# One kernel, one change: equal-width attention passes, high probabilities first, and the addition of the two halves moved behind the gate rows

## The chip, the cores and the metric

The kernel runs on one core of one Trainium2 chip. The metric is the device time of one execution in microseconds (us). TensorE does the matrix products, VectorE (DVE in the profile), ScalarE (ACT) and GpSimd (POOL) the work on elements, SyncE (SP) starts most transfers. Each engine takes its instructions in the order in which they are written; between engines only semaphores hold the order.

## The reference, cut to what matters

Eight sequences of 512 tokens with 256 features go through a state-space block (stage A), a mixture-of-experts attention with 16 heads of 64 features (stage B) and a feed-forward block (stage C). The change is in stage B:

```
q = rope(x Wq); k = rope(x Wk)
v = sum over experts e of gv[e] * (x Wv[e])
att = softmax(q k^T / 8)
o = att v
out = sum over experts e of (go[e] * o) Wo[e]
```

The products are kept near fp32 accuracy by splitting each operand into a high part (rounded for TensorE) and a low part (what the rounding left). A product is then high x high + high x low + low x high.

## The kernel before, in words

Stage B runs 64 times over one body: 8 pairs of heads (`j`) times 8 sequences (`b`), `it = 8 j + b`, called a batch here. Each engine has its own `batch` function, and these four lists of calls, written out by hand, are the schedule.

For one batch TensorE (`batch`, L1169) makes the values of both heads (`values`), the scores (`scores`), then transposes the probabilities of head 0 (`turn_probabilities`, L1107, n = 0 to 3), multiplies values by probabilities for head 0 (`attend`, L1124), does the same for head 1 (n = 4 to 7) with the transpose of the output gates between (`turn_gates`), spreads the gates over all partitions (`spread_gates` p = 0 to 3, L1138), with the next batch's q and k between them (`project_raw`), and ends with the eight steps of the output product (`project` n = 0 to 7, L1149). `project` n = 0 waits for `oT_low0`, the low part of the first gated output.

Each transposed block of probabilities is split: ScalarE writes the high part (`high_probabilities`, L1241), VectorE the low part (`low_probabilities`, L1366, waits for the high part). `probT` has four places, so head 1 uses those of head 0 again; ScalarE waits for `pv_psum` of the pass that read the place.

`attend` forms, for a head and a block c of 128 keys, two passes of 512 columns into one PSUM bank. The tile `vv` holds a head's values as 64 high columns and then 64 low columns. The pass with the high probabilities takes all 128 columns and so fills 128 PSUM partitions: high values in one half, low values in the other. The pass with the low probabilities takes only the 64 high columns and adds to the first half. Both wait until the low probabilities of block c are there:

```
pe.wait_ge(pT_low, it * N + n + 1)
```

The output of a head is the sum of the two halves of its bank. ScalarE copies one half to the partitions of the other, into the tile `aside` (`move_part`, L1251), and VectorE adds it (`add_parts`, L1378) into `oT`. `move_part` waits for the four passes of its head and for `oT_done`, which `add_parts` counts up:

```
act.wait_ge(pv_psum, it * N + h * TT + TT)
act.wait_ge(oT_done, it * 2 + h)
```

So `move_part` of head 1 comes behind `add_parts` of head 0.

VectorE's list for this part of a batch is: low probabilities 0 to 3, `output_gates`, one step of the ranking of gates (`tops`), `add_parts` of head 0, low probabilities 4 to 7, `low_gates` (L1371, the low part of the transposed gates, 16 rows from partition 64 on), `add_parts` of head 1, `gate_outputs` 0 and 1 (L1385, gate times `oT`), and more. `gate_outputs` 0 waits for both `add_parts`. ScalarE then makes `ogT_high` (`high_outputs`, L1258) and GpSimd `ogT_low` (`low_outputs`, L971) of the first four gated outputs, for which `project` waits.

GpSimd sums the gated expert values in `sum_values` (L956) through the tile `qk_full`, whose second half (`qk_full[:, 1, :]`) holds the sums of the later tokens (`v4`). `rotate` (L1330) writes the whole of `qk_full` for the next batch.

Of the kernel before, what the change touches and what calls it, by code (L numbers as in the profile page):

```python
# [15 lines left out]
F32, F32R = mybir.dt.float32, mybir.dt.float32r  # L16
ALU = mybir.AluOpType
ACT = mybir.ActivationFunctionType
AX = mybir.AxisListType

P = 128
NB, S, D = 8, 512, 256
TT = S // P
# [6 lines left out]
H, E, HP, F = 16, 8, 64, 1024  # L30
# [758 lines left out]
def stage_b(nc, d, const, acc):  # L789
# [6 lines left out]
    with ExitStack() as ctx:  # L796
        def sb(name, shape, dtype=F32):
            return ctx.enter_context(nc.sbuf_tensor(name, shape, dtype))
# [7 lines left out]
        ps = ctx.enter_context(nc.psum_tensor("ps_b", [P, 8, S], F32))  # L806
# [23 lines left out]
        qk_full = sb("qk_full", [P, 2, S])  # L830
# [1 line left out]
        vg = sb("vg", [P, TT, E, HP])  # L832

        v4 = qk_full[:, :, :].rearrange("p a s -> p (a s)").rearrange("p (t e n) -> p t e n", t=TT, e=E // 2)
        oT, aside = sb("oT", [P, S]), sb("aside", [P, S])
        v2 = sb("v2", [P, TT, E // 4, HP])
        v = sb("v", [P, 2, TT, HP])
        vv = sb("vv", [P, 2, TT, 2 * HP], F32R)
        negmax = sb("negmax", [P, TT, 2])
        total = sb("total", [P, 2, TT])  # L840
        share = sb("share", [P, 2, TT])
# [3 lines left out]
        RING = 4  # L845
# [22 lines left out]
        N = BLOCKS  # L868
# [58 lines left out]
        def turns(eng, start, batch, pair_start=None):  # L927

            def pair(j, more):
                if pair_start:  # L930
                    pair_start(j)
                with eng.Fori(0, NB - 1) as b:
                    batch(j * NB + b, j, b, True, False)
                batch(j * NB + (NB - 1), j, NB - 1, False, more)

            start()
            with eng.Fori(0, PAIRS - 1) as j:
                pair(j, True)
            pair(PAIRS - 1, False)

        @block.gpsimd
        def _(pool):
            def low_x(it):
                pool.wait_ge(xT_high, it + 1)
                pool.tensor_tensor(xT[1][:, :, :], xT_in[:, :, :], xT[0][:, :, :].bitcast(F32), ALU.subtract).then_inc(xT_low, 1)
# [20 lines left out]

            def low_values(it, h):
                pool.wait_ge(v_high, it * 2 + h + 1)
                pool.tensor_tensor(vv[:, h, :, HP:2 * HP], v[:, h, :, :], vv[:, h, :, 0:HP].bitcast(F32), ALU.subtract).then_inc(v_low, 1)

            def low_outputs(it, e):  # L971

# [85 lines left out]
                    rank_four(it + 1, ahead)  # L1058

            pool.memset(out_gate[:, :, :], 0.0).then_inc(zero_done, 1)  # L1060
            low_x(0)

            pool.dma_start(acc[:, :, :, :], d["xT"].rearrange("b p k s -> p b k s")).then_inc(acc_loaded, 16)
# [3 lines left out]
        def _(pe):  # L1067
# [53 lines left out]
                    mm = pe.transpose(ps[:, GT_BANK, t * P:(t + 1) * P], out_gate[:, t, :], ident[:, :])  # L1121
                mm.then_inc(gT_psum, 1)

            def attend(it, h, c):  # L1124

                if c == 0:
                    pe.wait_ge(v_low, it * 2 + h + 1)
                n = h * TT + c
                pe.wait_ge(pT_low, it * N + n + 1)
                bank, last = ATTEND_BANK[h], c == TT - 1  # L1130
                if last:
                    pe.matmul(ps[0:HP, bank, :], vv[:, h, c, 0:HP], probT[1][:, n % RING, :], start=False, stop=False)
                mm = pe.matmul(ps[:, bank, :], vv[:, h, c, :], probT[0][:, n % RING, :], start=(c == 0), stop=last)
                if not last:
                    mm = pe.matmul(ps[0:HP, bank, :], vv[:, h, c, 0:HP], probT[1][:, n % RING, :], start=False, stop=False)
                mm.then_inc(pv_psum, 1)

            def spread_gates(it, p):  # L1138

# [29 lines left out]
            def batch(it, j, b, more, more_pairs):  # L1169
                pe.wait_ge(w_low["wv"], j * 2 + 2)  # L1170
                values(it, 0, 0)
                values(it, 0, 1)
                scores(it, 0)
                scores(it, 1)
                values(it, 0, 2)
                values(it, 0, 3)
                values(it, 1, 0)
                scores(it, 2)
                scores(it, 3)
                values(it, 1, 1)  # L1180
                values(it, 1, 2)
                values(it, 1, 3)
                for n in range(TT):
                    turn_probabilities(it, n)
                for c in range(TT):
                    attend(it, 0, c)
                for n in range(TT, N):
                    turn_probabilities(it, n)
                turn_gates(it)
                for c in range(TT):  # L1190
                    attend(it, 1, c)
                spread_gates(it, 0)
                spread_gates(it, 1)
                if more or more_pairs:
                    if more_pairs:
                        pe.wait_ge(w_low["wqk"], j + 2)
                    project_raw(it + 1, 0)
                spread_gates(it, 2)
                if more or more_pairs:
                    project_raw(it + 1, 1)  # L1200
                spread_gates(it, 3)
                for n in range(N):
                    project(it, j, n)

            pe.wait_ge(consts_done, 1)
            turns(pe, start, batch)

        @block.scalar
        def _(act):
# [26 lines left out]

            def high_values(it, h):
                act.wait_ge(vsum_done, CREDIT + it * VSUM + h * 6 + 6)
                act.activation(vv[:, h, :, 0:HP], v[:, h, :, :], ACT.Copy).then_inc(v_high, 1)

            def high_probabilities(it, n):  # L1241
                act.wait_ge(pT_psum, it * N + n + 1)
# [74 lines left out]
        def _(dve):  # L1317
# [12 lines left out]
            def rotate(it):  # L1330

                dve.wait_ge(vsum_done, CREDIT + it * VSUM)
                dve.wait_ge(rot_done, it * 3 + 3)
                dve.tensor_tensor(qk_full[:, :, :], rot[:, 0:2, :], rot[:, 2:4, :], ALU.add).then_inc(qk_done, 1)

# [35 lines left out]
            def low_gates(it):  # L1371

                dve.wait_ge(gT_high, it + 1)
                rows = slice(LOW_ROW, LOW_ROW + 2 * E)
                low = gT[rows, :]
                dve.tensor_tensor(low, ps[rows, GT_BANK, :], low.bitcast(F32), ALU.subtract).then_inc(gT_low, 1)

            def add_parts(it, h):  # L1378

                here = slice(h * HP, (h + 1) * HP)  # L1380
                dve.wait_ge(part_moved, it * 2 + h + 1)
                dve.wait_ge(og_done, CREDIT + it * EP)
                dve.tensor_tensor(oT[here, :], ps[here, ATTEND_BANK[h], :], aside[here, :], ALU.add).then_inc(oT_done, 1)
# [37 lines left out]
            def batch(it, j, b, more, more_pairs):  # L1421
                coming = (it + 1, j if more else j + 1, b + 1 if more else 0)
                gate_values(it, j, b, 0)
                maxima(it, 0)
                maxima(it, 1)
                gate_values(it, j, b, 1)
                maxima(it, 2)
                maxima(it, 3)
                gate_values(it, j, b, 2)
                gate_values(it, j, b, 3)  # L1430
                for n in range(TT):
                    low_probabilities(it, n)
                output_gates(it)
                if more or more_pairs:
                    tops(*coming, 0)
                add_parts(it, 0)
                for n in range(TT, N):
                    low_probabilities(it, n)
                low_gates(it)
                add_parts(it, 1)  # L1440
                gate_outputs(it, 0)
                gate_outputs(it, 1)
                if more or more_pairs:
                    tops(*coming, 1)
                gate_outputs(it, 2)
                gate_outputs(it, 3)
                if more or more_pairs:
                    turn_raw(it + 1)
                low_outputs(it, 0)
                if more or more_pairs:  # L1450
                    swap_halves(it + 1)
                low_outputs(it, 1)
                if more:
                    tops(*coming, 2)
                if more or more_pairs:
                    rotate(it + 1)
                low_outputs(it, 2)
                low_outputs(it, 3)
                if more_pairs:
                    tops(*coming, 2)  # L1460
                    low_qk(it + 1)
                    tops(*coming, 3)
                elif more:
                    tops(*coming, 3)
                    low_qk(it + 1)
                dve.wait_ge(acc_loaded, 16)
                dve.wait_ge(out_psum, CREDIT + it * KD + KD)
                dve.tensor_tensor(acc[:, bass.ds(b, 1), :, :], acc[:, bass.ds(b, 1), :, :], ps[:, OUT:OUT + KD, :].unsqueeze(1),
                                  ALU.add).then_inc(acc_done, 1)

            dve.wait_ge(tables_loaded, 32)
            dve.wait_ge(consts_done, 1)
            dve.wait_ge(zero_done, 1)
            turns(dve, start, batch)


# [394 lines left out]
```

## Time and profile before

| | us |
|---|---|
| median of 3 runs | 4357.75 (4352.01 to 4357.77) |
| the profiled execution | 4360.78 |
| its span, first to last instruction | 4358.8 |
| TensorE busy | 3803.9 (87%) |
| VectorE busy | 3630.8 (83%) |
| GpSimd busy | 2849.6 (65%) |
| ScalarE busy | 2029.6 (47%) |
| mean granted TensorE clock over the span | 0.909 of 2.4 GHz |

Stage B lies between about 1450 and 4080 us of the span. A matmul is pipelined: the record of one lasts longer than the step to the next one's start, so steps are read from starts. An engine's "idle before" is the time since its last instruction ended, with the instruction that ended the wait. "issue" is idle time for which the profile shows no releaser.

### The profile page before, as it was taken

What the parts mean: (1) busy time and instruction counts of PE and PEld (TensorE: products, weight loads), DVE (VectorE), ACT (ScalarE), POOL (GpSimd) and SP (SyncE); (2) the same over time, 40 slices, a digit from 0 to 9 for tenths busy, and PEclk for the clock granted to TensorE, in tenths of its full rate; (3) what the DMA queues carried; (4) which work ended last, traced back from release to release, by engine and by line L of the source; (5) the groups of instructions that cost most, each with busy time, mean ns of one, the idle gap of its engine ahead of it and who ended that gap; (6) DMA issues with size and microseconds to landing.
All of it is one profiled execution on the core that took longest, in us unless ns stands there. A gap on an engine that the chain in (4) does not pass through costs nothing. (4 is left out here: it accounts for less than half of the span.)

```text
span 4358.8 us, 54031 instructions
## 1 busy us (share of the span) xinstructions
PE 3803.9 (87%) x15744; PEld 2541.1 (58%) x15744; DVE 3630.8 (83%) x4012; ACT 2029.6 (47%) x3761; POOL 2849.6 (65%) x2524
## 2 busy tenths in 40 slices
PE   6777867867765599999999999999999999999787
PEld 2233323323322377777777777777777777777676
DVE  5999999999998478877887887887888788778598
ACT  4544535535443244544444444444444444444433
POOL 2758668567594366766766766766766766766444
PEclk8877877877876799999999999999999999999898
DMA  1000000000000300100100100100100100000101
GB/s 39 0 10 15 24 5 19 24 5 19 15 5 20 131 13 12 41 14 10 41 14 10 41 14 10 41 14 10 41 14 10 41 14 10 20 14 15 31 29 44
DMA packets 48726, 97.83 MB, mean 22 GB/s; under 512 B 3570, under 2 KB 33138, under 8 KB 46228
## 3 DMA queue, kind: packets, MB, share of 16 engines
q1 hardware_dynamic: 47620, 92.94, 6.2%
q0 software_dynamic: 1040, 4.19, 0.2%
q8 instruction: 19, 0.31, 0.0%
q14 instruction: 47, 0.39, 0.0%
HBM read 80.34 MB, written 16.78 MB: 22 GB/s over the span
## 5 line engine op out<-in xcount | busy, mean ns | idle before, releaser
L702 DVE TENSOR_TENSOR_SCAN state<-dA,dBx 128x2048 f32<-128x2048 f32 x128 | 726.8, 5678 | 25.9 <-POOL y_part L289 21.3
L1234 ACT ACTIVATE prob<-ps_b,negmax 128x512 f32<-128x512 f32 x512 | 346.1, 687 | 652.3 <-DVE negmax L1353 652.3
L286 POOL TENSOR_TENSOR state<-state,c_copy 128x1024 f32<-128x1024 f32 x120 | 345.5, 2879 | 374.8 <-DVE state L702 374.8
L1347 DVE TENSOR_TENSOR vg<-ps_b,gates 128x1024 f32<-128x1024 f32 x256 | 313.5, 1224 | 253.1 <-PE ps_b L1072 241.1
L961 POOL TENSOR_TENSOR qk_full<-vg 128x512 f32<-128x512 f32 x256 | 329.0, 1285 | 253.3 <-DVE vg L1347 253.3
L549 ACT ACTIVATE dA<-dt,a_neg 128x511 f32<-128x511 f32 x512 | 326.9, 711 | 323.9 <-DVE state L702 323.7
L974 POOL TENSOR_TENSOR ogT_low<-prob,ogT_high 128x512 fp32r<-128x512 f32 x256 | 324.0, 1295 | 208.9 <-ACT ogT_high L1267 208.9
L372 PE MATMUL ps_a<-xp_high,ident_r 33*128 33x512 f32 x256 | 163.0, 637 | 332.6 <-DVE dBx L692 307.9
L1070 PE MATMUL ps_b<-ogT_high,wo_high 128*128 128x512 f32 x1024 | 413.2, 403 | 11.1 <-DVE ogT_low L1399 10.8
L1070 PE MATMUL ps_b<-wv_high,xT_high 128*128 128x512 f32 x1024 | 414.6, 405 | 0.0
L289 POOL TENSOR_TENSOR y_part<-y_part,state 128x1024 f32<-128x1024 f32 x120 | 403.4, 3362 | 9.4
L1072 PE MATMUL ps_b<-ogT_high,wo_low 128*128 128x512 f32 x1024 | 405.2, 396 | 0.0
L1071 PE MATMUL ps_b<-ogT_low,wo_high 128*128 128x512 f32 x1024 | 402.9, 393 | 0.0
L1071 PE MATMUL ps_b<-wv_low,xT_high 128*128 128x512 f32 x1024 | 401.5, 392 | 0.0
L1072 PE MATMUL ps_b<-wv_high,xT_low 128*128 128x512 f32 x1024 | 399.2, 390 | 0.0
L393 PE MATMUL ps_a<-state,ident 128*128 128x512 f32 x512 | 345.9, 813 | 24.8 <-DVE work L719 22.7
L1353 DVE TENSOR_REDUCE negmax<-ps_b 128x2 f32<-128x1024 f32 x256 | 301.0, 1217 | 62.8 <-PE ps_b L1103 62.8
L372 PEld LDWEIGHTS ps_a<-xp_high,ident_r 33*128 33x128 f32 x256 | 59.0, 231 | 495.5 <-DVE dBx L692 399.0
L1368 DVE TENSOR_TENSOR probT_low<-ps_b,probT_high 128x512 fp32r<-128x512 f32 x512 | 316.4, 677 | 2.3 <-ACT probT_high L1245 2.3
L1245 ACT ACTIVATE probT_high<-ps_b 128x512 fp32r<-128x512 f32 x512 | 264.7, 605 | 61.8 <-PE ps_b L1114 59.7
L692 DVE TENSOR_TENSOR dBx<-du,ps_a 128x2048 f32<-128x2048 f32 x128 | 289.0, 2258 | 1.8 <-PE ps_a L373 1.8
L1267 ACT ACTIVATE ogT_high<-ps_b 128x512 fp32r<-128x512 f32 x256 | 153.1, 598 | 242.0 <-PE ps_b L1072 242.0
(237 smaller groups left out, 9530.9 us busy)
## 6 DMA issues: line engine op xcount, KB each, us to landing
xT<-xT_scratch SPq DMA_DIRECT2D x65, 512.0 KB, 3.3
wv<-in_wv SPq DMA_DIRECT2D x8, 1024.0 KB, 4.9
wo<-in_wo SPq DMA_DIRECT2D x8, 1024.0 KB, 7.0
x_in<-in_x SPq DMA_DIRECT2D x8, 512.0 KB, 4.7
x_a<-in_x SPq DMA_DIRECT2D x8, 512.0 KB, 5.3
x_scratch<-x_a SPq DMA_DIRECT2D x8, 512.0 KB, 2.9
xT_scratch<-x2T SPq DMA_DIRECT2D x8, 512.0 KB, 2.6
scores_scratch<-sg SPq DMA_DIRECT2D x8, 512.0 KB, 3.5
```

The costliest lines, as they stand in the source:

```text
L286: pool.tensor_tensor(state, state, c, ALU.mult).then_inc(hc_part_done, 1)
L289: pool.tensor_tensor(y[:, :, :], y[:, :, :], state, ALU.add).then_inc(y_part_done, 1)
L393: mm = pe.matmul(ps[:, m, :], ident[:, :], h[n % 2][:, m, :], start=(n == 0), stop=(n == NS - 1))
L549: act.activation(dA[n % 2][:, m, 1:S], dt[par][:, m, 1:S], ACT.Exp, scale=a_neg[:, m, n:n + 1]).then_inc(dA_done, 1)
L702: dve.tensor_tensor_scan(h[n % 2][:, :, :].rearrange("p c s -> p (c s)"), dA[n % 2][:, :, :].rearrange("p c s -> p (c s)"), dBx[n % 2][:, ...
L961: pool.tensor_tensor(v4[:, at, :, :], vg[:, at, 0:4, :], vg[:, at, 4:8, :], ALU.add).then_inc(vsum_done, 1)
L974: pool.tensor_tensor(ogT[1][:, e, :], og[:, e, :], ogT[0][:, e, :].bitcast(F32), ALU.subtract).then_inc(oT_low0, 1)
L1070: pe.matmul(out, left(0), right(0), start=start, stop=False)
L1071: pe.matmul(out, left(0), right(1), start=False, stop=False)
L1072: return pe.matmul(out, left(1), right(0), start=False, stop=stop)
L1234: act.activation(prob[h][:, t, :], ps[:, score_bank(t) + h, :], ACT.Exp, bias=negmax[:, t, h:h + 1], accum_out=total[:, h, t:t + 1]).then_ ...
L1368: dve.tensor_tensor(probT[1][:, n % RING, :], ps[:, n % TT, :], probT[0][:, n % RING, :].bitcast(F32), ALU.subtract).then_inc(pT_low, 1)
```

## The change

The tile `vv` gets 64 more columns per block that are always zero, and its order becomes low, high, zero. The pass with the high probabilities takes low and high, that with the low probabilities high and zero, so all passes are 128 columns wide. `attend` does a whole head: four passes with the high probabilities, each waiting only for the high part of its block (`pT_high`), and then four with the low ones, each waiting for `pT_low`; each low pass counts `pv_psum`. As VectorE's progress is no longer implied by the first wait, `attend` waits for `vg_done` as well. `aside` has no tile of its own any more: it lies in the second half of `qk_full`, and `rotate` waits for `oT_done`. GpSimd zeroes the new columns once, and TensorE and VectorE wait for that at the start of the stage. On VectorE `add_parts` of head 0 moves from before low probabilities 4 to 7 to behind `low_gates`. `move_part` and `add_parts` themselves are as before.

```diff
-        oT, aside = sb("oT", [P, S]), sb("aside", [P, S])
+        oT, aside = sb("oT", [P, S]), qk_full[:, 1, :]
...
-        vv = sb("vv", [P, 2, TT, 2 * HP], F32R)
+        vv = sb("vv", [P, 2, TT, 3 * HP], F32R)
...
             def low_values(it, h):
                 pool.wait_ge(v_high, it * 2 + h + 1)
-                pool.tensor_tensor(vv[:, h, :, HP:2 * HP], v[:, h, :, :], vv[:, h, :, 0:HP].bitcast(F32), ALU.subtract).then_inc(v_low, 1)
+                pool.tensor_tensor(vv[:, h, :, 0:HP], v[:, h, :, :], vv[:, h, :, HP:2 * HP].bitcast(F32), ALU.subtract).then_inc(v_low, 1)
...
             pool.memset(out_gate[:, :, :], 0.0).then_inc(zero_done, 1)
+            pool.memset(vv[:, :, :, 2 * HP:3 * HP].bitcast(F32), 0.0).then_inc(zero_done, 1)
             low_x(0)
...
-            def attend(it, h, c):
-
-                if c == 0:
-                    pe.wait_ge(v_low, it * 2 + h + 1)
-                n = h * TT + c
-                pe.wait_ge(pT_low, it * N + n + 1)
-                bank, last = ATTEND_BANK[h], c == TT - 1
-                if last:
-                    pe.matmul(ps[0:HP, bank, :], vv[:, h, c, 0:HP], probT[1][:, n % RING, :], start=False, stop=False)
-                mm = pe.matmul(ps[:, bank, :], vv[:, h, c, :], probT[0][:, n % RING, :], start=(c == 0), stop=last)
-                if not last:
-                    mm = pe.matmul(ps[0:HP, bank, :], vv[:, h, c, 0:HP], probT[1][:, n % RING, :], start=False, stop=False)
-                mm.then_inc(pv_psum, 1)
+            def attend(it, h):
+
+                pe.wait_ge(v_low, it * 2 + h + 1)
+                pe.wait_ge(vg_done, it * 4 + 3)
+                bank = ATTEND_BANK[h]
+                for c in range(TT):
+                    pe.wait_ge(pT_high, it * N + h * TT + c + 1)
+                    pe.matmul(ps[:, bank, :], vv[:, h, c, 0:2 * HP], probT[0][:, c % RING, :], start=(c == 0), stop=False)
+                for c in range(TT):
+                    pe.wait_ge(pT_low, it * N + h * TT + c + 1)
+                    pe.matmul(ps[:, bank, :], vv[:, h, c, HP:3 * HP], probT[1][:, c % RING, :], start=False, stop=(c == TT - 1)).then_inc(pv_psum, 1)
...
-                for c in range(TT):
-                    attend(it, 0, c)
+                attend(it, 0)
                 for n in range(TT, N):
                     turn_probabilities(it, n)
                 turn_gates(it)
-                for c in range(TT):
-                    attend(it, 1, c)
+                attend(it, 1)
...
             pe.wait_ge(consts_done, 1)
+            pe.wait_ge(zero_done, 2)
...
             def high_values(it, h):
                 act.wait_ge(vsum_done, CREDIT + it * VSUM + h * 6 + 6)
-                act.activation(vv[:, h, :, 0:HP], v[:, h, :, :], ACT.Copy).then_inc(v_high, 1)
+                act.activation(vv[:, h, :, HP:2 * HP], v[:, h, :, :], ACT.Copy).then_inc(v_high, 1)
...
             def rotate(it):
 
                 dve.wait_ge(vsum_done, CREDIT + it * VSUM)
+                dve.wait_ge(oT_done, it * 2)
...
-                add_parts(it, 0)
                 for n in range(TT, N):
                     low_probabilities(it, n)
                 low_gates(it)
+                add_parts(it, 0)
                 add_parts(it, 1)
                 gate_outputs(it, 0)
...
-            dve.wait_ge(zero_done, 1)
+            dve.wait_ge(zero_done, 2)
```

## Rows read from the trace of the kernel before

**Rows 1.** Busy time by stretch: PE, PEld, DVE, ACT, POOL, clock, DMA, GB/s.
```profile
1700.00:4200.00 2500.00, 2431.05 (x11816) 1817.19 (x11814) 1986.33 (x2603) 1192.93 (x2420) 1710.45 (x2002) 0.99 0.06 22
```

**Rows 2.** Waits between 1704.58 and 4023 us: total us, times, longest.
```profile
PEld ps_b L1133 <- DVE probT_low L1368: 130.3, 348, 1.4
```

**Rows 3.** TensorE in order of time, one batch: start us, us, operation.
```profile
3001.99 1.91 PE L1114 MATMUL ps_b<-ident,prob 128*128 128x128 f32 x16
...
3006.13 0.45 PE L1132 MATMUL ps_b<-probT_low,vv 128*64 128x512 f32 x1
3006.41 0.40 PE L1133 MATMUL ps_b<-probT_high,vv 128*128 128x512 f32 x1
3006.85 1.20 PE L1147 MATMUL ps_b<-gT,spread 128*128 128x512 f32 x4
...
3011.13 0.63 PE L1147 MATMUL ps_b<-gT,spread 128*128 128x512 f32 x2
3011.69 0.47 PE L1070 MATMUL ps_b<-ogT_high,wo_high 128*128 128x512 f32 x1
```

**Rows 4.** What ended TensorE's idle time before L1147: us, times.
```profile
  DVE gT L1376: 30.4, 64
```

**Rows 5.** VectorE in order of time, the same batch.
```profile
2998.95 2.48 DVE L1368 TENSOR_TENSOR probT_low<-ps_b,probT_high 128x512 fp32r<-128x512 f32 x4
...
3003.00 0.68 DVE L1383 TENSOR_TENSOR oT<-ps_b,aside 64x512 f32<-64x512 f32 x1 [0.79 <-ACT aside L1256]
3003.61 2.47 DVE L1368 TENSOR_TENSOR probT_low<-ps_b,probT_high 128x512 fp32r<-128x512 f32 x4
3006.11 0.69 DVE L1376 TENSOR_TENSOR gT<-ps_b,gT 16x512 fp32r<-16x512 f32 x1
3007.55 0.69 DVE L1383 TENSOR_TENSOR oT<-ps_b,aside 64x512 f32<-64x512 f32 x1 [0.76 <-ACT aside L1256]
```

**Rows 6.** ScalarE in order of time, the same batch.
```profile
2998.17 2.07 ACT L1245 ACTIVATE probT_high<-ps_b 128x512 fp32r<-128x512 f32 x4 [1.05 <-PE ps_b L1114]
...
3001.81 0.42 ACT L1239 ACTIVATE vv<-v 128x256 fp32r<-128x256 f32 x1 [0.63 <-POOL v L965]
3002.27 0.60 ACT L1256 ACTIVATE aside<-ps_b 64x512 f32<-64x512 f32 x1
3002.89 2.07 ACT L1245 ACTIVATE probT_high<-ps_b 128x512 fp32r<-128x512 f32 x4
...
3006.93 0.59 ACT L1256 ACTIVATE aside<-ps_b 64x512 f32<-64x512 f32 x1 [1.47 <-PE ps_b L1133]
3009.53 2.28 ACT L1267 ACTIVATE ogT_high<-prob 128x512 fp32r<-128x512 f32 x4 [2.02 <-DVE prob L1392]
```

**Rows 7.** GpSimd between 3010.3 and 3011.3 us.
```profile
3010.24 1.30 POOL L974 TENSOR_TENSOR ogT_low<-prob,ogT_high 128x512 fp32r<-128x512 f32 x1 [3.24 <-ACT ogT_high L1267]
```

**Rows 8.** GpSimd, then TensorE, in the last batch, between 4059 and 4062 us.
```profile
4060.10 2.55 POOL L974 TENSOR_TENSOR ogT_low<-prob,ogT_high 128x512 fp32r<-128x512 f32 x2 [4.70 <-ACT ogT_high L1267]
...
4061.54 0.47 PE L1070 MATMUL ps_b<-ogT_high,wo_high 128*128 128x512 f32 x1 [0.26 <-POOL ogT_low L974]
```

**Rows 9.** Weight loads of L1132 and L1133: ns min/median/max, first and last start.
```profile
L1132 PEld LDWEIGHTS ps_b<-probT_low,vv x128: 132/133/133, 1508.3 to 4056.1; 128*64 128x64 f32 x128
...
L1133 PEld LDWEIGHTS ps_b<-probT_high,vv x512: 186/186/189, 1506.5 to 4056.1; 128*128 128x128 f32 x171
```

**Rows 10.** GpSimd in order of time at the start of stage B.
```profile
1447.04 0.52 POOL L1060 MEMSET out_gate<- 128x512 f32 x1 [34.49 <-POOLq L123]
1455.42 2.34 POOL L945 TENSOR_TENSOR xT_low<-xT,xT_high 128x1024 fp32r<-128x1024 f32 x1 [7.85 <-ACT xT_high L1213]
```

**Rows 11.** ScalarE, then VectorE, in a pair's first batch, 3443.9 to 3445 us.
```profile
3443.86 0.60 ACT L1245 ACTIVATE probT_high<-ps_b 128x512 fp32r<-128x512 f32 x1
...
3444.49 0.69 DVE L1368 TENSOR_TENSOR probT_low<-ps_b,probT_high 128x512 fp32r<-128x512 f32 x1 [0.34 <-ACT probT_high L1245]
```

**Rows 12.** VectorE between 3008.3 and 3009.3 us, the batch of rows 5.
```profile
3008.28 1.22 DVE L1392 TENSOR_TENSOR prob<-oT,ps_b 128x1024 f32<-128x1024 f32 x1
```

## The prediction, made before the result was known

> **What bounds the kernel now.** I read the page first: its busy shares and its list of groups. The change touches stage B alone. By stretches, TensorE is busy 2431 of 2500 us there at a granted clock of 0.99, that is at its upper level, 2.4 GHz, while VectorE has 1986 us [rows 1]. So a batch (64 of them, some 40 us each) lasts as long as TensorE's passes plus its few stalls, and the question is which stalls the change shortens or adds. The list of waits names the ones aimed at: passes of L1133 waiting for low probabilities, 130.3 us over 348 times, as weight loads [rows 2].
>
> Next I followed one batch in order of time, TensorE, VectorE, ScalarE and GpSimd side by side. The reader is to see that what ends each stall is a chain through other engines, not the passes:
>
> - Head 0: VectorE's fourth low part ends at 2998.95 + 2.48 = 3001.43, and TensorE goes on to the transposes of head 1 at 3001.99 [rows 3, 5].
> - ScalarE's `move_part` of head 0 starts at 3002.27, right behind the rounding of head 1's values, and that waited for GpSimd's sum [rows 6]. Not the attention passes but the value sums set when it starts. Then come ScalarE's high parts 4 to 7, from 3002.89.
> - VectorE: `add_parts` 0 from 3003.00 to 3003.68, low parts 4 to 7 from 3003.61 to 3006.08, `low_gates` from 3006.11 to 3006.80 [rows 5]. TensorE's gate spreading starts at 3006.85 [rows 3]; it waited for `low_gates` in all 64 batches, 30.4 us [rows 4]. The last pass of head 1, started at 3006.41, was early enough.
> - The second half: ScalarE `move_part` 1 from 3006.93 to 3007.52, VectorE `add_parts` 1 at 3007.55, `gate_outputs` 0 at 3008.28, `ogT_high` at 3009.53, GpSimd's `ogT_low` from 3010.24 to 3011.54, `project` at 3011.69 [rows 3, 5, 6, 7, 12].
> - Is that last wait real? TensorE's previous pair of passes, 3011.13 with 0.63 us in all, starts its second pass 0.23 us after its first (a record lasts 0.40 us) and would let `project` begin at 3011.13 + 2 x 0.23 = 3011.59. It began 0.10 us later, 0.15 us after GpSimd's end. In the last batch, where TensorE has nothing else to do, the trace names this releaser: GpSimd ends at 4060.10 + 1.30 = 4061.40 and `project` starts 0.14 us later [rows 7, 8]. The same handing over, so `project` is held by this chain in every batch, with TensorE only 0.10 us behind it.
>
> **The change part by part.**
>
> *Order of the passes.* Head 0: the fourth low part still ends at 3001.43; one pass stands behind it where there were two, so the transposes begin at most one step (0.23 us) sooner. Nothing downstream takes that up: `move_part` 0 is held by GpSimd's sums. I take 0; the ends are 0 and -0.23 us a batch. Head 1: the last pass is released by the fourth low part and followed by none, but the gates' spreading waits for `low_gates` anyway. The new waits: `vg_done` 3 and `v_low` are over long before, so they cost 0.
>
> *Width.* A low pass now loads 128 columns of weights, 186 ns for 133 [rows 9]; only loads that follow a wait are exposed, and at most the difference, 0.05 us, for each head. It falls in front of `low_gates`' end, so 0.
>
> *Zeroing and tile.* A fill of 512 elements per partition takes 0.52 us, once, and GpSimd then idles 7.85 us for ScalarE [rows 10]: 0; uncovered it would be 0.5 us in all. `rotate` comes some 10 us after `add_parts` 1 on its own engine: 0. `aside` in `qk_full` is written by ScalarE after the last value sum: 0.
>
> *`add_parts` 0 behind `low_gates`.* This is the dear part. Ahead of it there is a small gain: low part 4 no longer waits behind the addition, but for its high part, which ends at 3002.89 + 0.60 = 3003.49. A low part that waits only for that starts 0.03 us after it (3443.86 + 0.60 = 3444.46, then 3444.49) [rows 11]. So 3003.52 for 3003.61; the four end at 3005.99, `low_gates` at 3006.02 + 0.69 = 3006.71, and TensorE's spreading starts near 3006.76, 0.09 us sooner.
>
> Behind it stands a loss. `move_part` 1 still waits for `add_parts` 0, which so far was long done, and which now comes last:
> - `add_parts` 0 behind `low_gates`: 3006.71 + 0.03 = 3006.74, ends at 3007.42 (0.68 us).
> - ScalarE takes it up 0.03 us later (`gate_outputs` 0 ends at 3008.28 + 1.22 = 3009.50, `ogT_high` starts at 3009.53) [rows 6, 12]: `move_part` 1 from 3007.45 to 3008.04. Its passes have been over since about 3006.5.
> - `add_parts` 1 0.03 us later, at 3008.07 instead of 3007.55: **0.52 us late**.
>
> Behind `move_part` 1 in ScalarE's order are only the `high_outputs`, which need its result anyway. From `add_parts` 1 to `project` everything is a chain of the same lengths: `gate_outputs` 0, `ogT_high`, `ogT_low` move by 0.52, and `project` starts at 3012.21. The gate spreading p = 3 waits for `gate_outputs` 1, at most 3008.28 + 2 x 1.22 + 0.52 = 3011.24, and is through by 3011.9; it is not the last. Behind `project` 0 the passes follow each other, so all else shifts with it. Cost: 64 x 0.52 = 33.3 us.
>
> *Both ends of the unknowns.* The step from `low_gates` to `add_parts` 0 isn't in the trace. Low parts that follow each other start 0.07 us before the one in front ends (four of 0.67 us in 2.47: a step of 0.60); `low_gates` behind a low part started 0.03 us after its end, and `gate_outputs` 0 behind `add_parts` 1 at 3008.24 + 0.04 [rows 5, 12]. In these two the start partition changes, from 0 to 64 and back, as it will here. So 0.03; with the overlap the batch costs 0.42 us and the sum is 27 us. The Trainium skill, "VectorE: DVE Perf Modes", section "Two Vector instructions with no wait between them", says that an instruction whose inputs or output start in another quadrant than the last ones starts only when all earlier ones have finished; the trace agrees (0.03 us after the end against 0.07 before it), and by the page the sum is 33 us where free overlap would give 27. Handing over from ScalarE took 0.03 us for `move_part` 1 but 0.13 for `move_part` 0 (3002.87 to 3003.00) [rows 5, 6]. I take 0.03, since `move_part` 1 is the same instruction with ScalarE idle behind it; two such dearer steps would make 0.72 us, 46 us. If TensorE were not ready for `project` on time it would change nothing, for it is ready 0.6 us before.
>
> **The sum.** The profiled execution took 4360.78 us, 3.03 above the median. 4360.78 + 33.3 = 4394.1, and by the median 4357.75 + 33.3 = **4391 us**.
>
> **The rivals.**
>
> *TensorE's order decides (faster).* TensorE has the highest busy share, so passes that no longer wait in pairs should tell. In head 1 the last pass would be released near 3006.05 and the spreading could begin near 3006.38 rather than at 3006.41 + 0.23 = 3006.64: 0.26 us, 64 x 0.26 = 17 us, 4341. This holds if neither `low_gates` nor GpSimd's end really releases TensorE. Against it: 64 waits out of 64 at L1147, and the named releaser in the last batch. It decides as soon as the chain behind `add_parts` 1 has over 0.6 us of slack.
>
> *The late addition is hidden (no change).* GpSimd's spans are rough; if `project` were held by something else than `ogT_low`, the 0.52 us would vanish and the 0.09 us before the spreading remain: 4357.75 - 6 = 4352. For it speaks that the trace files this wait of TensorE's under "issue" in ordinary batches; against it the equal 0.15 and 0.14 us.
>
> *Dearer handings over (slower still).* 0.13 us at both of ScalarE's ends: 4404.
>
> *The clock.* TensorE idles some 0.9 us more per batch in single stalls of up to 0.7 us. Were a tenth of each batch's passes granted 1.2 GHz, some 4 us of steps would double: over 250 us in all. In this stretch the clock stayed at 0.99 with stalls of 0.3 to 0.5 us each batch, so I give it little.
>
> **How the numbers follow.** Forecast 0.80 (own range 4384 to 4398), dearer steps 0.05, clock 0.02, hidden 0.07, faster 0.06. A measurement of this kernel can tell about 0.2% (8.7 us) from no change. Slower by more: 0.80 + 0.05 + 0.02 = 0.87; within: 0.07; faster by more: 0.06. The range for 8 in 10 takes the forecast's own range, the dearer steps as far as 4402, and some room below for a part that is hidden: 4379 to 4402.
>
> **What would show it.** `add_parts` 1 starting 9.12 us after the batch's first low part (3008.07 - 2998.95) where it was 8.60, `move_part` 1 released by VectorE's `oT` instead of TensorE; `low_gates` ending 0.09 us sooner; the first `ogT_low` 0.5 us late and TensorE's wait at L1070 growing from 0.10 to near 0.7 us; a batch of 40.5 us. The prediction is wrong if `project` starts on time although `ogT_low` is late, if the clock row falls, or if `move_part` 1 isn't released by `add_parts` 0.

## The result, and the profile after

| | before | after |
|---|---|---|
| median, us | 4354.9 (4352.01 to 4357.77, 4 runs) | 4387.41 (4385.64 to 4390.99, 4 runs) |
| profiled execution, us | 4360.78 | 4386.21 |
| its span, us | 4358.8 | 4384.0 |

The ratio is 1.0076, 95% interval 1.0058 to 1.0093: 33 us slower (25 to 41). The forecast was +33.3 us and 4391; the 4391 stood on the median of three runs, 4357.75, and by the median in this table the same 33.3 us give 4388.

Read the profile after in the same order. First VectorE in order of time over one batch (start, length in us, operation; "L1367" is `low_probabilities`, L1375 `low_gates`, L1382 `add_parts`, L1391 `gate_outputs`):

```profile
3013.26 2.48 DVE L1367 TENSOR_TENSOR probT_low<-ps_b,probT_high 128x512 fp32r<-128x512 f32 x4
...
3017.83 2.48 DVE L1367 TENSOR_TENSOR probT_low<-ps_b,probT_high 128x512 fp32r<-128x512 f32 x4 [1.31 <-ACT probT_high L1243]
3020.34 0.69 DVE L1375 TENSOR_TENSOR gT<-ps_b,gT 16x512 fp32r<-16x512 f32 x1
3021.06 0.68 DVE L1382 TENSOR_TENSOR oT<-ps_b,qk_full 64x512 f32<-64x512 f32 x1
3022.40 0.69 DVE L1382 TENSOR_TENSOR oT<-ps_b,qk_full 64x512 f32<-64x512 f32 x1 [0.66 <-ACT qk_full L1254]
```

Beside [rows 5], counted from the batch's first low part: the four low parts of head 1 start at 4.57 us (4.66 before), `low_gates` ends at 7.77 (7.85), and `add_parts` 1 starts at 9.14 (8.60; forecast 9.12). The small gain in front and the large loss behind it are both there. Who holds `add_parts` 1 is seen on ScalarE:

```profile
3016.13 0.42 ACT L1237 ACTIVATE vv<-v 128x256 fp32r<-128x256 f32 x1 [0.64 <-POOL v L965]
3016.58 0.59 ACT L1254 ACTIVATE qk_full<-ps_b 64x512 f32<-64x512 f32 x1
3017.20 2.06 ACT L1243 ACTIVATE probT_high<-ps_b 128x512 fp32r<-128x512 f32 x4
...
3021.78 0.59 ACT L1254 ACTIVATE qk_full<-ps_b 64x512 f32<-64x512 f32 x1 [2.03 <-DVE oT L1382]
```

`move_part` 1 starts at 3021.78, 0.04 us after `add_parts` 0 ends (3021.06 + 0.68), and its releaser is VectorE's `oT`; before it was TensorE's last pass [rows 6]. By the totals of the line:

```profile
L1254 ACT ACTIVATE qk_full<-ps_b x128: 589/594/597, 1503.9 to 4085.6; 64x512 f32<-64x512 f32 x128
its engine sat idle before it (us, times) until:
  DVE oT L1382: 129.8, 64
```

All 64 times the new wait ended last. On TensorE (L1132 the passes with high, L1135 those with low probabilities, L1146 the spreading, L1071 the first pass of `project`):

```profile
3018.22 1.58 PE L1132 MATMUL ps_b<-probT_high,vv 128*128 128x512 f32 x4
3019.65 1.22 PE L1135 MATMUL ps_b<-probT_low,vv 128*128 128x512 f32 x4
3021.09 1.20 PE L1146 MATMUL ps_b<-gT,spread 128*128 128x512 f32 x4 [0.22 <-DVE gT L1375]
...
3025.54 0.72 PE L1146 MATMUL ps_b<-gT,spread 128*128 128x512 f32 x2
3026.53 0.47 PE L1071 MATMUL ps_b<-ogT_high,wo_high 128*128 128x512 f32 x1 [0.27 <-POOL ogT_low L974]
```

The passes of head 1 end sooner (their last starts by 3020.4, 1.4 us before `move_part` 1), and nothing comes of it. `project` now waits visibly: GpSimd's `ogT_low` is the named releaser, where the trace before filed the wait under "issue" [rows 3, 8]. By the totals of L1071 it is the releaser in all 64 batches:

```profile
  POOL ogT_low L974: 16.9, 64
```

Last, the stretch as a whole: `low_gates` first and last start.

```profile
L1375 DVE TENSOR_TENSOR gT<-ps_b,gT x64: 689/689/690, 1507.7 to 4084.1; 16x512 fp32r<-16x512 f32 x64
```

From the first to the last of its 64 the kernel before took 4056.0 - 1512.9 = 2543.1 us and this one 2576.4: 33.3 us more in 63 batches, 0.53 each. The spans differ by only 25.2 us because the rest, whose code is the same but for one fill, was 8 us shorter in this profiled run. In what follows this distance ("first to last gate") is the measure in a trace.

Busy times and granted clock (the third column from the end) over nearly all batches, of the kernel before and then after:

```profile
1510.00:4040.00 2530.00, 2492.28 (x12026) 1851.20 (x12024) 2022.77 (x2570) 1206.30 (x2473) 1762.55 (x2103) 1.00 0.06 20
1510.00:4040.00 2530.00, 2482.93 (x11877) 1864.04 (x11876) 2001.77 (x2536) 1193.36 (x2447) 1742.33 (x2077) 1.00 0.06 20
```

The clock is 1.00 in both: in the profiled executions the added stalls cost none. Over the whole span it was 0.908 to 0.910 in three of the four runs after, and 0.87 in the fourth, which took 4390.99 us, 2.4 more than the next; that run has no trace, so where its clock was lower isn't known.

### The profile page after: what moved, and what is told of

Same layout as the page of the kernel before. It is cut to its first block and busy times, and to the rows that moved or that the text cites. A ratio compares the mean times of both kernels' runs of the same rounds, so it can differ in the third digit from the quotient of the medians.

```text
span 4384.0 us, 54159 instructions
## 1 busy us (share of the span) xinstructions
PE 3829.7 (87%) x15744; PEld 2578.2 (59%) x15744; DVE 3628.0 (83%) x4012; ACT 2030.9 (46%) x3761; POOL 2854.5 (65%) x2525
## 5 line engine op out<-in xcount | busy, mean ns | idle before, releaser
L1071 PE MATMUL ps_b<-ogT_high,wo_high 128*128 128x512 f32 x1024 | 409.4, 400 | 27.7 <-POOL ogT_low L974 16.9
L1071 PE MATMUL ps_b<-wv_high,xT_high 128*128 128x512 f32 x1024 | 414.4, 405 | 0.0
L1367 DVE TENSOR_TENSOR probT_low<-ps_b,probT_high 128x512 fp32r<-128x512 f32 x512 | 317.5, 683 | 91.1 <-ACT probT_high L1243 91.1
L393 PE MATMUL ps_a<-state,ident 128*128 128x512 f32 x512 | 355.4, 832 | 24.8 <-DVE work L719 22.6
```

The lines of the kernel that those rows point to most:

```text
L393: mm = pe.matmul(ps[:, m, :], ident[:, :], h[n % 2][:, m, :], start=(n == 0), stop=(n == NS - 1))
L1071: pe.matmul(out, left(0), right(0), start=start, stop=False)
L1367: dve.tensor_tensor(probT[1][:, n % RING, :], ps[:, n % TT, :], probT[0][:, n % RING, :].bitcast(F32), ALU.subtract).then_inc(pT_low, 1)
```

## The experiments

The theory: the whole cost is that `move_part` 1 waits for `add_parts` 0. The rivals: the passes (their order or width) or the shared tile cost something; or the place of the addition on VectorE costs by its own length.

**e1: the addition back in its place.**

```diff
+                add_parts(it, 0)
                 for n in range(TT, N):
                     low_probabilities(it, n)
                 low_gates(it)
-                add_parts(it, 0)
                 add_parts(it, 1)
```

> The changed kernel with add_parts 0 back before low probabilities 4 to 7; passes, zero columns and tiles stay changed. Theory (the late addition in front of move_part 1 is the whole cost): add_parts 1 starts 8.60 us after the batch's first low part again, project 1 starts as in the kernel before, time within 0.2% of the kernel before, about 4355 to 4358 us. Rival (the order or the width of the passes, or the shared tile, costs something): it stays slower, 4370 us or more. Rival (the passes themselves gain): up to 6 us under the kernel before, since the low parts of head 1 are held by add_parts 0 and TensorE was only 0.10 us behind the chain.

Measured: 4343.36 us (10 runs), ratio to the kernel before 0.9976 (0.9967 to 0.9986), -10 us. The loss is gone, so passes, zero columns and tile carry none of it. But the kernel is now faster than the one before, by more than the 6 us that I had allowed for, and first to last gate is 4040.0 - 1508.3 = 2531.7 us, 11.4 less than before. ScalarE and TensorE show from where:

```profile
2990.65 0.42 ACT L1237 ACTIVATE vv<-v 128x256 fp32r<-128x256 f32 x1 [0.65 <-POOL v L965]
...
2991.71 2.07 ACT L1243 ACTIVATE probT_high<-ps_b 128x512 fp32r<-128x512 f32 x4
...
2995.55 0.59 ACT L1254 ACTIVATE qk_full<-ps_b 64x512 f32<-64x512 f32 x1 [1.28 <-PE ps_b L1135]
```

```profile
2994.17 1.27 PE L1135 MATMUL ps_b<-probT_low,vv 128*128 128x512 f32 x4
2995.66 1.20 PE L1146 MATMUL ps_b<-gT,spread 128*128 128x512 f32 x4 [0.23 <-DVE gT L1375]
...
2999.94 0.63 PE L1146 MATMUL ps_b<-gT,spread 128*128 128x512 f32 x2
3000.41 0.40 PE L1071 MATMUL ps_b<-ogT_high,wo_high 128*128 128x512 f32 x1
3000.64 0.39 PE L1072 MATMUL ps_b<-ogT_low,wo_high 128*128 128x512 f32 x1
```

`move_part` 1 starts 3.84 us after the high parts of head 1 do; before it was 3006.93 - 3002.89 = 4.04 [rows 6]. With one pass instead of two behind the last low part, it is released 0.2 us sooner. And `project` follows the spreading without a wait: it starts 0.47 us after the last two passes of the spreading do, not 0.56 [rows 3], its record is 0.40 us long, not 0.47, and the next pass follows it after 0.23 us. In the kernel before that step was 0.31 us, 3011.69 to 3012.00; I take the difference for a weight load that only a released pass leaves exposed. The two savings make 0.17 us a batch, of 0.18 by the gates. The new pass order by itself is worth some 10 us, and on top of the new passes the moved addition costs 4387.41 - 4343.36 = 44 us.

**e2: the kernel before with the one edit that e1 undid** (`add_parts` 0 behind `low_gates`, passes in pairs).

> The kernel before with one edit: add_parts 0 behind low_gates; passes in pairs as before. Theory: the same loss as the whole change, 0.53 us a batch, +34 us, about 4389 us, and project released by GpSimd's ogT_low. Rival (the new passes are part of the loss): less than half of it, under 4372 us.

Measured: 4389.87 us (4 runs), ratio 1.0085 (1.0070 to 1.0101), +36 us, and the wait is the same:

```profile
3024.60 0.59 ACT L1256 ACTIVATE aside<-ps_b 64x512 f32<-64x512 f32 x1 [2.03 <-DVE oT L1383]
```

One moved line of VectorE's list is enough for the whole loss. With that line moved the new passes are worth nothing: first to last gate is 4087.4 - 1510.0 = 2577.4 us here and 2576.4 after the change.

**e3: the wait taken away, the addition left late.** The two halves of `aside` lie in different partitions, and `move_part` 0 has already waited for the batch before.

```diff
-                act.wait_ge(oT_done, it * 2 + h)
+                if h == 0:
+                    act.wait_ge(oT_done, it * 2)
```

> The changed kernel, with move_part 1 no longer waiting for add_parts 0 (the two use different partitions of the tile, and move_part 0 has waited for the batch before on the same engine). Theory: the loss is that wait and not the place of the addition: move_part 1 starts when the passes of head 1 end, before add_parts 0 does, and add_parts 1 follows add_parts 0 at once, some 0.1 us earlier in the batch than in the kernel before; 0.05 to 0.10 us a batch gained, 4349 to 4355 us. Rival (the late addition costs by its own length on VectorE): add_parts 1 later than before, 4365 us or more.

Measured: 4358.39 us (11 runs), ratio 1.0006 (0.9997 to 1.0015): 29 us are back, and the time is that of the kernel before. The rival's 4365 us or more did not come; the few us under the kernel before that I had expected did not come either.

```profile
3002.13 0.69 DVE L1376 TENSOR_TENSOR gT<-ps_b,gT 16x512 fp32r<-16x512 f32 x1
3002.85 1.41 DVE L1383 TENSOR_TENSOR oT<-ps_b,qk_full 64x512 f32<-64x512 f32 x2
3004.30 2.35 DVE L1392 TENSOR_TENSOR prob<-oT,ps_b 128x1024 f32<-128x1024 f32 x2
```

```profile
2997.93 0.42 ACT L1237 ACTIVATE vv<-v 128x256 fp32r<-128x256 f32 x1 [0.64 <-POOL v L965]
...
3002.70 0.59 ACT L1255 ACTIVATE qk_full<-ps_b 64x512 f32<-64x512 f32 x1 [1.15 <-PE ps_b L1135]
3005.63 0.63 ACT L1266 ACTIVATE ogT_high<-prob 128x512 fp32r<-128x512 f32 x1 [2.34 <-DVE prob L1392]
```

`move_part` 1 now runs while VectorE does `low_gates`, and the two additions follow each other. `gate_outputs` 0 (1.22 us) ends at 3005.52, but `ogT_high` starts 0.11 us later, not 0.03: there the expected gain went (see e8).

The place of the addition is not free, though. The right kernel to hold e3 against is e1, which has the same passes and the addition early, and e3 is 15 us slower (4358.39 against 4343.36; by the gates 2544.4 against 2531.7 us). Counted from the rounding of head 1's values (`vv`), `gate_outputs` 0 starts at 6.37 us here and at 6.25 in e1, where it starts at 2996.90: two additions in a row behind `low_gates` take longer than waiting for `move_part` 1 does. With the dearer handing over `ogT_low` is 0.19 us later, and it holds `project` again in every batch. So of the 44 us that the moved addition costs with the new passes, 29 are the wait and 15 its place.

**e5: the addition in front of `low_gates`.**

```diff
                 for n in range(TT, N):
                     low_probabilities(it, n)
+                add_parts(it, 0)
                 low_gates(it)
-                add_parts(it, 0)
                 add_parts(it, 1)
```

> The changed kernel with add_parts 0 before low_gates instead of behind it. Theory (two chains end in a batch: low_gates releases the spreading and with it TensorE's work up to project, add_parts 0 releases move_part 1): add_parts 1 comes about 0.2 us earlier in the batch than in the kernel before, but low_gates 0.55 us later, so TensorE reaches project late: +0.45 us a batch, about 4383 us, with no wait on ogT_low. Rival (TensorE has slack in front of project and only the chain through oT counts): as fast as the kernel before or up to 10 us faster.

Measured: 4377.66 us (4 runs), ratio 1.0053 (1.0038 to 1.0069), +23 us.

```profile
3011.37 2.48 DVE L1367 TENSOR_TENSOR probT_low<-ps_b,probT_high 128x512 fp32r<-128x512 f32 x4 [1.32 <-ACT probT_high L1243]
3013.77 0.67 DVE L1382 TENSOR_TENSOR oT<-ps_b,qk_full 64x512 f32<-64x512 f32 x1
3014.48 0.69 DVE L1375 TENSOR_TENSOR gT<-ps_b,gT 16x512 fp32r<-16x512 f32 x1
3015.15 0.69 DVE L1382 TENSOR_TENSOR oT<-ps_b,qk_full 64x512 f32<-64x512 f32 x1
```

```profile
3015.22 1.20 PE L1146 MATMUL ps_b<-gT,spread 128*128 128x512 f32 x4 [0.81 <-DVE gT L1375]
...
3019.47 0.63 PE L1146 MATMUL ps_b<-gT,spread 128*128 128x512 f32 x2
3019.94 0.40 PE L1071 MATMUL ps_b<-ogT_high,wo_high 128*128 128x512 f32 x1
```

Now the other chain holds: the spreading starts late, and `project` follows it without a pause. So two chains end at `project`, close together, and this addition hurts in front of either. The loss was smaller than expected, 0.32 us a batch by the gates (2563.5 us) for 0.45. Some 0.07 of that is the step behind `project`'s first pass, 0.24 us (3019.94 to 3020.18) where it is 0.31 when a wait releases it; the rest is that `low_gates` and the work to `project` came a little less late than I had reckoned.

**e4: a better order of ScalarE's list**, on top of e3.

```diff
-                move_part(it, 0)
                 for n in range(TT, N):
                     high_probabilities(it, n)
                 high_gates(it)
+                move_part(it, 0)
                 move_part(it, 1)
```

> As the kernel with the free move_part 1, and ScalarE does the high parts 4 to 7 and the gates before move_part 0. Theory (the chain from ScalarE's high parts 4 to 7 through VectorE to ogT_low sets each batch, and TensorE has 0.3 us or more of slack there): the high parts start 0.4 to 0.5 us sooner, when the transposes are there; low_gates, gate_outputs 0 and project come about 0.5 us sooner than in the kernel before; -30 to -36 us, about 4320 us. Rival (TensorE's passes would be late then): project is held by TensorE, gain under 15 us, 4340 us or more.

Measured: 4326.53 us (5 runs), ratio 0.9938 (0.9925 to 0.9952), -27 us (21 to 33): 3 us outside the expectation, the mechanism as expected.

```profile
2980.24 0.42 ACT L1237 ACTIVATE vv<-v 128x256 fp32r<-128x256 f32 x1 [0.65 <-POOL v L965]
2980.86 2.07 ACT L1243 ACTIVATE probT_high<-ps_b 128x512 fp32r<-128x512 f32 x4 [0.20 <-PE ps_b L1115]
2982.78 0.63 ACT L1247 ACTIVATE gT<-ps_b 128x512 fp32r<-128x512 f32 x1
2983.44 0.60 ACT L1255 ACTIVATE qk_full<-ps_b 64x512 f32<-64x512 f32 x1
```

The high parts start 0.62 us after the rounding of the values, 1.07 after the change, and are released by TensorE's transposes: the chain now begins at the passes of head 0. It still ends at `ogT_low`: `project` starts 0.14 to 0.15 us behind it in every batch.

**e6: e4 with narrow low passes**, 64 columns in three of four (the last keeps the zero columns).

```diff
...
+                    if c < TT - 1:
+                        pe.matmul(ps[0:HP, bank, :], vv[:, h, c, HP:2 * HP], probT[1][:, c % RING, :], start=False, stop=False).then_inc(pv_psum, 1)
...
```

> The kernel with high parts first, but three of a head's four passes with low probabilities are 64 columns wide again (the last keeps its zero columns). Theory (the width costs and saves nothing, the order does the work): within 4 us of the run e4, about 4326 us. Rival (changing the width between passes costs, or wider loads cost): 6 us or more away from it, in either direction.

Measured: 4328.03 us (5 runs), ratio 0.9939 (0.9925 to 0.9953), the same as e4; by the gates 2513.4 us against 2513.2. In this schedule the width is worth nothing either way.

**e7: the kernel before with e4's schedule but the old pairs of passes.**

> The kernel before with everything of e4 but the passes: add_parts 0 behind low_gates, move_part 1 free, high parts 4 to 7 first, passes in pairs that wait for the low part. Theory (in this schedule the start of head 1's transposes sets the high parts, and pairs end 0.17 us later in head 0 and 0.3 us later in head 1, of which add_parts 0 hides the latter): 0.17 us a batch slower than e4, about 4337 us. Rival (the order of the passes never matters): equal to e4 within 4 us.

Measured: 4338.11 us (5 runs), ratio 0.9963 (0.9949 to 0.9976), 11.6 us behind e4 (10.1 by the gates, 0.16 a batch), as expected.

```profile
2986.12 0.42 ACT L1239 ACTIVATE vv<-v 128x256 fp32r<-128x256 f32 x1 [0.65 <-POOL v L965]
2986.91 2.07 ACT L1245 ACTIVATE probT_high<-ps_b 128x512 fp32r<-128x512 f32 x4 [0.37 <-PE ps_b L1114]
```

Here the high parts wait for the transposes until 0.79 us after the rounding: the 0.17 us by which pairs end later in head 0, once nothing else stands in front, are paid in full.

**e8: e4 with a wait that is always fulfilled in front of `move_part` 1**, for the 0.11 us.

```diff
+                else:
+                    act.wait_ge(pT_psum, it * N + N)
```

> e4 with a wait in front of move_part 1 that has always been fulfilled by then (the last transposes of the batch), so that ScalarE has as many instructions as in the changed kernel. In e3 and e4 ScalarE took up gate_outputs 0 after 0.11 us instead of 0.03. If the number or place of ScalarE's instructions does that: the handing over is 0.03 us again, project 0.08 us sooner, 5 us under e4, about 4321 us. If it comes from VectorE doing add_parts 1 without a pause: it stays at 0.11 us and the time within 2 us of e4.

Measured: 4325.94 us (5 runs), ratio 0.9934 (0.9920 to 0.9947): no change. `gate_outputs` 0, then `ogT_high`, in a middle batch and in the last:

```profile
2990.46 1.22 DVE L1394 TENSOR_TENSOR prob<-oT,ps_b 128x1024 f32<-128x1024 f32 x1
...
2991.80 0.64 ACT L1268 ACTIVATE ogT_high<-prob 128x512 fp32r<-128x512 f32 x1 [2.35 <-DVE prob L1394]
...
4028.32 1.22 DVE L1394 TENSOR_TENSOR prob<-oT,ps_b 128x1024 f32<-128x1024 f32 x1
...
4029.57 0.63 ACT L1268 ACTIVATE ogT_high<-prob 128x512 fp32r<-128x512 f32 x1 [2.26 <-DVE prob L1394]
```

0.12 us in the middle, 0.03 in the last. The number of ScalarE's instructions isn't the cause. Nor is it enough that VectorE does the two additions without a pause, since the last batch has that too; and it isn't needed, since e9 has the 0.11 to 0.12 us with a pause of 0.13 us between the additions. The cause stays open.

**e9: the transposes of head 1 between the low passes of head 0**, on top of e4.

```diff
-                attend(it, 0)
-                for n in range(TT, N):
-                    turn_probabilities(it, n)
+                attend_high(it, 0)
+                for c in range(TT - 1):
+                    turn_probabilities(it, TT + c)
+                    attend_low(it, 0, c)
+                attend_low(it, 0, TT - 1)
+                turn_probabilities(it, N - 1)
...
+                high_probabilities(it, TT)
                 high_values(it, 1)
-                for n in range(TT, N):
+                for n in range(TT + 1, N):
                     high_probabilities(it, n)
```

> e4, and TensorE puts the transposes of head 1's blocks 4, 5 and 6 between head 0's passes with low probabilities, where it waits for VectorE; ScalarE does the high part of block 4 before it rounds head 1's values. Theory (the chain starts at the transposes of head 1): high parts 4 to 7 end 0.6 us sooner in the batch than in e4, the low parts and all behind them 0.7 us, project too, since TensorE is ready 0.15 us earlier than needed in e4 and gets all its own work sooner as well: 4326 - 64 x 0.7 = about 4280 us. Rival (another engine holds by then, the rounding of head 1's values or GpSimd): a gain under 20 us, 4306 us or more.

Measured: 4285.33 us (5 runs), ratio 0.9839 (0.9826 to 0.9853): 70 us faster than the kernel before, 102 less than the changed one, and 41 less than e4, where 46 were expected (36.9 by the gates).

```profile
2957.13 0.60 PE L1115 MATMUL ps_b<-ident,prob 128*128 128x128 f32 x4
2957.49 0.48 PE L1136 MATMUL ps_b<-probT_low,vv 128*128 128x512 f32 x1
2957.80 0.60 PE L1115 MATMUL ps_b<-ident,prob 128*128 128x128 f32 x4
```

Transposes and low passes fill each other's waits. The run joins two edits, TensorE's order and the early high part of block 4 on ScalarE, and doesn't tell what each is worth alone; `ogT_low` still releases `project` in every batch. Of the versions run, this is the one to keep.

## Why the prediction was right

- *The late addition, 0.52 us a batch:* right in mechanism, place and size (0.53 by the gates, 0.54 by `add_parts` 1). e2 shows that it suffices. Without it (e1) or without the wait behind it (e3) the kernel is no slower than before. The 33 us are a net of two terms, though: against e1 the late addition costs 44 us, 29 by the wait and 15 by its place, and the new passes give 10 back. The sum needed neither number: once `add_parts` 0 comes last, the chain through it sets `project` whatever the passes do, and that chain is what the working followed.
- *The gain in front, 0.09 us:* right (4.57 for 4.66 us); it ends at `low_gates`, as said.
- *The step from `low_gates` to `add_parts` 0:* 3021.06 against an end at 3021.03, so 0.03 us and not an overlap. ScalarE took up the addition after 0.04 us and VectorE the moved half after 0.03. The dearer handing over did not come, and nothing in the working said where it would: e3 met one.
- *The order of the passes at 0:* right for the sum, because the new wait hid it (e2 and the change are 1.0 us apart by the gates), but the working missed a term. I held the end of head 1's passes against `low_gates` only; it also released `move_part` 1. e1 shows that the term is worth some 10 us where it isn't hidden, and my expectation of e1 repeated the omission.
- *Width, tile, zeroing at 0:* e1 shows that together they cost nothing that can be seen, e6 the same of the width.
- *The rivals:* "TensorE's order decides" failed on `low_gates`, which still releases the spreading (0.22 us of idle PE in the rows above). "Hidden" failed, as `ogT_low` is the named releaser of `project`. The clock stayed in the profiled execution.
- *The signs:* `add_parts` 1 at 9.14 us for 9.12, `ogT_low` 0.55 us late, its releasers as said. Two were off, and the sum hung on neither. The batch of "40.5 us" was a slip: 2543.1 / 63 = 40.4 us before and 0.52 more are 40.9, as measured. And TensorE's wait in front of `project` grew to some 0.44 us, not 0.7, because the last two passes of the spreading had by then waited for `gate_outputs` 1: they start at 3025.54, `gate_outputs` 1 ends at 3025.48. TensorE was ready later than the working had it, but still in time.

## What to carry to other kernels

A wait that was always fulfilled costs nothing until the instruction that fulfils it is moved: look for every counter that a moved instruction raises, and for who waits on it. Shorter waits on the busiest engine pay only if that engine's next release comes sooner too; here the same pass order was worth 0, 10 or 12 us depending on what stood behind it. And where two chains end within a tenth of a microsecond of each other, price an edit on both.

## What the runs showed of the hardware

- On VectorE, in these rows, an instruction whose operands start at another partition than those of the one before it started 0.03 to 0.04 us after that one's end; with the same start it began before the end. e5 has both: `add_parts` 0 (partition 0, behind a low part) 0.08 us before the end, `low_gates` (64) 0.04 us after, `add_parts` 1 (64) 0.02 us before. The Trainium skill, "VectorE: DVE Perf Modes", section "Two Vector instructions with no wait between them", states it by the quadrants (32 partitions each) in which inputs and output start: another quadrant than before, and the instruction starts only when all earlier ones have finished. These rows agree with it.
- A handing over between VectorE and ScalarE, from the end of one to the start of the other, took 0.03 to 0.04 us in most places and 0.11 to 0.13 in two: `move_part` 0 to `add_parts` 0 in the kernel before and e1, `gate_outputs` 0 to `ogT_high` in e3, e4 and e6 to e9. Each has it in 63 batches and 0.03 in the last. e3 lost its expected 5 us by one of these. What sets it is open.
- Other handings over were the same in nearly every batch: ScalarE to GpSimd 0.08 us (`ogT_high` to `ogT_low`), GpSimd to TensorE 0.14 to 0.15 (`ogT_low` to `project`), each from the end by the profile.
